# Cross-attention chunk: both blocks of maxima and scores first, the projection piece last

## The reference, cut to what matters

```
q = layernorm(x) @ Wq.T + bq ; k = ctx @ Wk.T + bk ; v = ctx @ Wv.T + bv
scores = einsum('bhtd,bhcd->bhtc', q, k) / sqrt(16)     # t: 512, c: 1601
attn = softmax(scores) ; out = attn @ v
x = x + out @ Wo.T + bo
```

## Time and profile before

| | |
|---|---|
| times of 3 runs | 2066.85, 2073.86, 2075.45 us; median 2073.86 |
| profiled execution | 2066.13 us, of which the span from first to last instruction 2064.3 us |
| busy share of the span | PE 93%, PEld 48%, DVE 74%, ACT 59%, POOL 22% |
| TensorE clock | 0.952 of full speed on the mean |

### The profile page before, as it was taken

One profiled execution on the slowest core, in us unless ns is written; L12 is line 12 of the kernel. 1 busy time (PEld: TensorE's weight loads), 2 busy tenths in 40 slices (PEclk: granted clock), 3 DMA queues, 4 the chain that ended last, 5 costly groups with the idle time before them and its releaser, 6 DMA issues. The chain is left out here.

```text
span 2064.3 us, 35376 instructions
## 1 busy us (share of the span) xinstructions
PE 1919.6 (93%) x11964; PEld 989.6 (48%) x11964; DVE 1521.3 (74%) x3097; ACT 1209.5 (59%) x2439; POOL 448.3 (22%) x540
## 2 busy tenths in 40 slices
PE   6889886779999999999999999999999998699999
PEld 4656564534434444444443443444444332477875
DVE  6888886478888788778778777878877892455345
ACT  2232230137777777777777777777777777224541
POOL 1110012112211310211221221131121100026675
PEclk9999998669999999999999999999999999569999
DMA  5000000550540522253173064053234200314564
GB/s 185 1 0 0 0 0 5 115 127 1 122 111 13 116 65 64 77 105 65 43 133 70 1 145 94 7 110 72 65 85 96 33 2 1 132 45 141 165 198 129
DMA packets 67406, 151.81 MB, mean 74 GB/s; under 512 B 12385, under 2 KB 39009, under 8 KB 67105
## 3 DMA queue, kind: packets, MB, share of 16 engines
q1 hardware_dynamic: 60432, 131.18, 27.3%
q0 software_dynamic: 6816, 18.62, 3.3%
HBM read 95.80 MB, written 53.23 MB: 72 GB/s over the span
## 5 line engine op out<-in xcount | busy, mean ns | idle before, releaser
L1155 DVE TENSOR_REDUCE x_mx<-x_ps 128x1 f32<-128x512 f32 x1536 | 976.2, 685 | 215.3 <-PE x_ps L900 205.9
L1060 ACT ACTIVATE x_probs<-x_ps 128x512 f32<-128x512 f32 (+1 forms) x1664 | 894.3, 597 | 282.7 <-PE x_ps L964 276.7
L964 PE MATMUL x_ps<-x_qst,x_kst 50*128 50x512 f32 (+1 forms) x1664 | 597.7, 454 | 23.5 <-ACT x_probs L1060 21.3
L900 PE MATMUL x_ps<-x_kst,x_qst 48*128 48x512 f32 x1536 | 573.2, 461 | 16.9 <-DMA x_kst<-k_parts 11.0
L948 PE MATMUL x_ps<-x_probs,x_vst 128*17 128x512 f32 (+1 forms) x3328 | 449.0, 612 | 4.8 <-ACT x_ou L1043 4.8
L900 PEld LDWEIGHTS x_ps<-x_kst,x_qst 48*128 48x128 f32 x1536 | 239.9, 191 | 432.8 <-DVE x_mx L1155 286.7
L964 PEld LDWEIGHTS x_ps<-x_qst,x_kst 50*128 50x128 f32 (+1 forms) x1664 | 243.7, 184 | 119.3 <-ACT x_probs L1060 105.3
L1092 POOL TENSOR_TENSOR x_vst<-x_v_all,x_bv 128x768 f32<-128x768 f32 x64 | 66.5, 1071 | 379.0 <-ACT x_v_all L1018 300.4
L284 ACT ACTIVATE r_qwide<-r_qT,r_headmask 128x512 f32<-128x512 f32 x128 | 80.0, 709 | 105.0 <-DVE r_qT L433 105.0
L213 PE MATMUL r_ps<-r_qwide,r_kT 128*128 128x512 f32 x256 | 116.3, 602 | 10.0 <-DVE r_vz L439 10.0
L886 PE MATMUL x_ps<-x_ctxT,x_wk 128*128 128x256 f32 (+1 forms) x448 | 123.5, 402 | 0.0
(11 more groups left out here) (211 smaller groups left out, 2125.9 us busy)
## 6 DMA issues: line engine op xcount, KB each, us to landing
x_kst<-k_parts SPq DMA_DIRECT2D x192, 200.1 KB, 8.4
k_parts<-x_kp SPq DMA_DIRECT2D x16, 1601.0 KB, 5.7
x_ctxT<-in_ctxT SPq DMA_DIRECT2D x8, 1601.0 KB, 8.1
x_qst<-q_parts SPq DMA_DIRECT2D x192, 64.0 KB, 2.6
sorted_y<-f_yt SPq DMA_DIRECT2D x26, 384.0 KB
q_parts<-x_qp SPq DMA_DIRECT2D x8, 1024.0 KB, 4.3
x_all<-in_x SPq DMA_DIRECT2D x8, 512.0 KB, 4.0
rows_x<-f_xn SPq DMA_DIRECT2D x8, 512.0 KB, 5.6
```

Of the source, the lines that this page charges most:

```text
L900: m = pe.matmul(o, qst[mg][rows, pair, t * P:(t + 1) * P], kst[mg][rows, pair, i * 512:(i + 1) * 512], start=True, stop=True)
L964: pe.matmul(ps[0:w, n % S_BANKS, :], kst[g][rows, pair, c * P:c * P + w], qst[g][rows, pair, :], start=True, stop=True).then_inc(s_filled, 1)
L1060: nc.scalar.activation(probs[0:w, s % (2 * GH), :], ps[0:w, s % S_BANKS, :], ACT.Exp, scale=HD ** -0.5).then_inc(exp_done, 1)
L1155: nc.vector.tensor_reduce(out=mx[:, 2 * pair + half, t, i:i + 1], in_=o, axis=AX.X, op=ALU.max).then_inc(drained_v, 1)
```

## The change

The order within a chunk becomes: block 1, block 2, weighted sums of the chunk before, piece. The plan's tuple is turned round, TensorE's loop follows it, and so do the drains on ScalarE: a piece is now drained behind the chunk's fourth exponential instead of its second. VectorE follows the plan's order without an edit, and so do the banks of `STREAM`. No instruction is added or taken away.

```
 def work_of(...)
-    return [[(first[g][c], pieces[g][c], second[g][c]) for c in range(SC)] for g in range(G)]
+    return [[(first[g][c], second[g][c], pieces[g][c]) for c in range(SC)] for g in range(G)]
...
 TensorE, in each chunk
-                        first, pieces, second = PLANS[b][g][c]
+                        first, second, pieces = PLANS[b][g][c]
                         n = woven(b, g, c, 0, n, first)
-                        for i in range(len(pieces)):
-                            fill(b, n + i, g)
-                        n = woven(b, g, c, 1, n + len(pieces), second)
+                        n = woven(b, g, c, 1, n, second)
                         if c:
                             values(b, g, c - 1)
                         elif b or g:
                             values(b - (g == 0), (g - 1) % G, SC - 1)
+                        for i in range(len(pieces)):
+                            fill(b, n + i, g)
+                        n += len(pieces)
...
 ScalarE, behind the exponentials of each pair
-                            for item in [item for part in PLANS[b][g][c][2 * pair:2 * pair + 2] for item in part]:
+                            for item in [item for part in PLANS[b][g][c][pair:2 * pair + 1] for item in part]:
```

## The result

The changed kernel takes 2183.74 us (median of 4 runs, 2178.30 to 2196.32) against 2070.83 (2066.85 to 2075.45): a ratio of 1.0553, with a 95% interval of 1.0495 to 1.0611. Forecast was 2180, slower. The profiled execution took 2188.73 us, its span 2186.9 against 2064.3; times and granted clocks differ from run to run, so the profiled pair is 122.6 us apart and the medians 112.9.

What follows compares the result with a forecast made beforehand. TensorE was taken to bound chunks with a piece, its parts following without a wait; losing the piece's cover over the score-bank wait added 114.5 us to the profiled 2066.1, giving 2180 us, range 2155 to 2210 for 8 in 10.

Steps and rivals of the forecast that it cites:

- ordinary piece and shift: Chunks with q, k, v, xnT, oT, wo at chunk 7 or shift: +0.32 us each, 247 of them, 79.0 us.
- chunk 1 with a piece: At chunk 1 the sums' wait for ScalarE's copy is no longer hidden: +0.87 us each, 21 times, 18.3 us.
- chunk 8 with a piece: At chunk 8, where the tails stand in block 2 behind the waiting score: +0.53 us each, 11.1 us.
- norm at chunk 2: At chunk 2, where tails in block 1 already cover part of the exponential: +0.17 us each, 30 times, 5.1 us.
- Its difference is the same: In ordinary chunks, a piece of any length, shift's 0.34 us included, moves with its own length: +0.32 us.
- The pieces' boundary: Weighted sums to piece, unseen in the trace: taken as costing the same; 0.07 us either way would make 22 us.
- What I cost at nothing: ScalarE's piece drains, VectorE, GpSimd and SyncE work, work-bank reuse and the shift's later end: nothing added.
- The shift's way to the next group: Drain and four DMAs before the next group's scores: 4.88 us needed, 5.60 left; a miss some 5 us.
- The drain's fit: ScalarE's piece drain before a chunk's first exponential: starts 0.17 us in, exponential 0.40 us later, nothing added.
- the third rival: ScalarE's later piece drain delays first exponential and fourth score: 0.1 us in 290 chunks is 29 us (2209); 12 in 100.
- The clock rival: TensorE's clock falls more often with waits: 15 us at five batch starts, 78 at every chunk 1; 6 in 100.
- The faster rival: Blocks back to back save an array layout change if the fourth score's bank is free: 52 us less, 2014; 4 in 100.

Runs made afterwards that it cites:

- the first experiment: The changed kernel with the piece moved between the second block and the weighted sums (blocks, piece, sums): 2174.09 us.

## Why the prediction was right

To set the terms against the chip I took the start of every chunk's first score in both profiles and summed the changes by kind, 121.9 us in all:

| kind | chunks | forecast, each and sum | measured, median and sum |
|---|---|---|---|
| ordinary piece and shift | 248 | 0.32, 79.0 | 0.31 (shift 0.28), 77.1 |
| chunk 1 with a piece | 21 | 0.87, 18.3 | 0.87, 18.3 |
| chunk 8 with a piece | 21 | 0.53, 11.1 | 0.54, 11.4 |
| norm at chunk 2 | 31 | 0.17, 5.1 | 0.15, 4.9 |
| no piece | 94 | 0 | 0.00, 10.2 |

The forecast sums leave out 1 us for the two pieces in chunks without maxima; they are counted with their kinds on the measured side.

- **The step that carried it**, reading the new chunk off the chunk without a piece and adding the piece's own time, held to 0.02 us in the median of each kind but the shift. That the wait is the score bank's is shown from three sides. A bank less lengthens the chunk by one exponential in the new order and not at all behind a "k", "q" or "v" piece in the old one; shorter exponentials shorten the wait; and in every "k" chunk of the changed kernel the weights of the fourth score load 0.05 us after the first exponential ends, while in the kernel before they load 0.19 to 0.68 us after it.
- **"Its difference is the same"** for a piece of any length was not quite right: a chunk with a shift grew by 0.28 us. Its 0.34 us did not cover the wait: in the kernel before, too, the fourth score's weights load 0.05 us after the exponential there.
- **The pieces' boundary** was given 22 us either way; it needed none, as the profile after and the first experiment show.
- **"What I cost at nothing"** held in the main. The shift's way to the next group did: no stall of the kind in rows 9 appeared at the later groups. The drain's fit did behind "k", "q" and "v" pieces, whose drain rows 4 show. Behind xnT, oT and shift pieces the drain takes 0.59 to 0.60 us and not 0.47 or less. Here it stands behind an xnT piece, in the chunk that starts at 1030.68 (xnT is kept in the tile of oT):

```profile
1030.84 0.60 ACT L1024 ACTIVATE x_oT<-x_ps 128x512 f32<-128x512 f32 x1 [0.79 <-PE x_ps L873]
1031.34 2.04 ACT L1061 ACTIVATE x_probs<-x_ps 65x512 f32<-65x512 f32 x4
```

The first exponential starts 0.66 us into the chunk and not 0.56, so the chunk behind such a piece grew by 0.07 to 0.10 us (by 0.03 behind oT), some 4 us in all. That is the third rival, by ScalarE, in small. In the first experiment, where the piece ends earlier, the exponential starts at 0.56 to 0.57 behind all pieces.
- **A wait that shrank** was not counted either: at chunk 6 of batch 0 the first "v" piece waits for the load of the context, 4.64 us before and 1.91 after, as block 2 and the sums now come first. That chunk became 3.2 us shorter, and with the 4 us above it nearly cancels in the first row of the table.
- **What was left out** is most of the 10.2 us in chunks that did not change. Some 9 of them are clock. The two falls at the starts of batches 2 and 5 are gone, worth some 6 us (4 of them in the row of the norms). But one came at the start of batch 7, some 5 us, and the last group, which has neither maxima nor, but for one norm, pieces, fell to 1.2 GHz at its chunk 2 instead of its chunk 7. In batch 0 chunks 7 and 8, at 0.58 on the mean from 464 to 477 us, took 2.7 us more. The last 0.7 of the 10.2 are the chunks behind ten of the shifts. The windows of the changed kernel over the start of batch 7 and over the last group from its chunk 2 on, then of the kernel before over the last group's chunks 0 to 6 and its end:

```profile
1722.00:1737.00 15.00, 14.27 (x72) 5.47 (x64) 8.76 (x17) 7.52 (x16) 2.09 (x2) 0.57 0.61 89
1843.00:1887.00 44.00, 41.15 (x140) 10.62 (x136) 0.68 (x2) 22.64 (x44) 0.00 (x0) 0.51 0.00 1
```

```profile
1724.73:1743.00 18.27, 15.07 (x92) 4.76 (x88) 0.68 (x2) 14.60 (x30) 0.00 (x0) 1.00 0.00 0
1743.00:1769.00 26.00, 24.05 (x88) 5.38 (x80) 0.00 (x0) 12.92 (x26) 0.00 (x0) 0.54 0.00 1
```

The clock rival was thus right in kind, at the price of one fall more or less in a run and not at each chunk 1. What sets a fall in one place and not in the same place of another batch stays open. That 2180 came within 4 us of the median is in part luck: runs of the kernel before differ by more than that, and the forecast started from one of the fastest.
- **The faster rival** failed by its condition: the fourth score does not find its bank free. Its size, 0.18 us, stays open. With the shortest exponentials the saving was 0.06 us: the fourth pair came 0.27 behind the third and the sums 0.42 behind that, where the rival had 0.24 and 0.33. But there the fourth score's weights still wait for the exponential, so 0.06 us, or 17 us over 291 chunks, is what that run shows and not what a free bank would give.

## What to carry to other kernels

Work that sits between two steps of a chain is not idle filling: before moving it, look what finishes under it, and find the stage in the profile that already runs without it, because that stage shows the new time. A pair of producers with fewer banks than steps between them waits for the consumer somewhere; moving the cover moves the wait, and there must be as much cover as there are pairs.

## What was not expected of the hardware

In the kernel before and the changed one TensorE's clock fell to 1.2 GHz in places where the engine had not been idle for more than about half a microsecond at a time, in stretches of chunks without pieces, at some batch starts and not at others of the same instructions; one such fall at a batch start cost about 3 us in the kernel before and some 5 in the changed one. Seventeen runs of the kernel before on one chip differed by up to 25 us (2059.82 to 2084.74, with mean clocks of 0.952 and 0.941 at the two ends), the four of the changed kernel by 18 (2178.30 to 2196.32, 0.954 and 0.943). And a change that makes TensorE wait can cost in clock a good part of what it costs in waits: two score banks in the old order took 102 us more than the kernel before on the same chip (2181.93 against 2079.43, one run each). By the chunks that had the full clock the waits make some 57 of these, 34 in chunks without a piece and 23 behind the shorter pieces. What is left is put down to the clock; the last group of the two-bank kernel hardly had the full clock, so what waits there are in it cannot be told apart.
